# The tail of a two-layer network kernel: y in four 1 MB loads, x1 fetched earlier, four PSUM banks, sixteen result rooms

## The chip, the cores and the metric

The kernel runs on one core of a Trainium2 chip. The metric is the device time of one execution in microseconds; the number given for a kernel is the median of several runs. Beside it there is one profiled execution, whose instructions and transfers are recorded; its span is the time from its first to its last instruction.

## The reference

Two layers, each with a residual. Cut to what matters:

```
x  = x + L0_ffn(L0_cond(x))          # layer 0: (32, 128, 2048), a mixed 128x128 product, then 2048x2048 with LoRA
# layer 1, in the kernel: x1 is the x after layer 0
z  = conv1d_groups4_9taps(x1) + context + bias         # (32, 128, 2048)
t  = z.reshape(4096, 2048)[:, perm] -> (4096, 16 heads, 128)
t  = gelu(t @ up[h]) @ down[h]                         # 128 -> 512 -> 128 for each head
y  = t.reshape(4096, 2048)[:, unperm]
out = x1 + y.reshape(32, 128, 2048)
```

All arithmetic is fp32; products are made as three TensorE products of a high and a low part.

## The kernel before

**Layer 1 in blocks and steps.** The 4096 rows (32 batches of 128 channels) are worked in 8 blocks (`BLOCKS`) of 512 rows, that is 4 batches. A block has 16 steps (`H`), one for each head. In step (k, h) TensorE makes the down products of head h and, between them, the up products of the next head (`down_part` L1336, `up_part` L1326); ScalarE makes gelu and copies y out of PSUM; VectorE splits values into high and low parts (`split_g` L1558, `split_t` L1513). GpSimd gathers the rows of z of a later head from DRAM through the permutation (L1268) and scatters the head's 128 x 512 rows of y to `y_d` in DRAM (L1303). The conv of a later block runs 20 steps ahead (`LEAD`), so the last block has none.

**Final units.** Adding x1 to y and storing is cut into units of one batch and 512 columns, 16 for a block; 256 KB each of y, x1 and output. As y of a block is complete only when its 16 scatters have landed, the units of block k-1 run within block k: SyncE loads y (`load_final`, L1179) and x1 (L1182) two units ahead, TensorE turns y with four 128x128 transposes (`turn_y`, L1371), VectorE adds x1 with a change of the order of columns (`take_final`, L1537), SyncE stores (`store_out`, L1210). SyncE's queue is worked in program order: in each step first a load of the last units' x1 (below), then `load_final`, then `store_out` of two units before. `load_final` of unit v waits for the transposes of v-2 (`fin_done`) and for the sum of v-2 (`o_ready`).

**The tail.** The 16 units of the last block have nothing to hide in. `last_unit(v)` goes through them batch by batch: batch v // 4, columns v % 4.
- x1 (`last_x1[v]`): 7 rooms that are free in the last block are filled by `load_last_x1` (L1192), one in each of its steps 0 to 6, and the other 9 by GpSimd after its last scatter (L1313): four at once into the rooms of gelu, the rest as sums free the first rooms.
- y (`finish`, L1204): after all scatters have landed (wait at L1202), one load of 256 KB for each unit, `y_d[c*512:(c+1)*512, 128 columns]`, so rows of 512 bytes, in a ring of 4 rooms; each waits for the transposes of the unit before its room's last use.
- TensorE turns a unit with four transposes (L1398) into one of two PSUM banks, VectorE adds (L1590) into one of four result rooms, and ScalarE's queue stores it (L1481). A sum waits until the store of the unit four before has landed.

The weights of layer 1 lie in SBUF throughout, as 8 tiles `w_hi[c]` and 8 `w_lo[c]` of 128 x 4 x 512; tile c holds the up and down chunks of heads 2c and 2c+1. So in the last block tile c is read for the last time in step 2c+1.

Of the kernel before, what the change touches and what calls it, by code (L numbers as in the profile page):

```python
# [967 lines left out]
def layer1_block(nc, sh, x1_d, up, down, perm, ident, z_d, y_d, out):  # L968

    with ExitStack() as ctx:  # L970
# [47 lines left out]
        x1_in = [sem(f"x1f_in{j}") for j in range(2)]  # L1018
        fin_done, o_ready = sem("fin_done"), sem("o_ready")
        o_out = [sem(f"o_out{j}") for j in range(2)]  # L1020
        last_x1_in = [sem(f"last_x1_in{v}") for v in range(H)]
        last_yt_in, last_o_out = [sem(f"last_yt_in{j}") for j in range(4)], [sem(f"last_o_out{j}") for j in range(4)]
        last_fin, last_o = sem("last_fin"), sem("last_o")
        block = ctx.enter_context(nc.Block())

# [20 lines left out]
        def drive(eng, step):  # L1046
# [11 lines left out]
            for k in (BLOCKS - 2, BLOCKS - 1):  # L1058
# [3 lines left out]
            step(BLOCKS, 1, 0)  # L1062


        left = ([sh.x1_s[:].rearrange("p a n -> p (a n)")[:, n * 512:(n + 1) * 512] for n in range(4)]
                + [xp[j][:, 0:512] for j in range(2)] + [z_s[:]])
        last_x1 = left + [g_s[:, mc, :] for mc in range(MC)]
        ROOMS = len(last_x1)
        last_x1 = (last_x1 + last_x1)[:H]
        last_x1 = [room.rearrange("p (s q) -> p s q", s=S) for room in last_x1]  # L1070
        last_yt = yt_s + [t.rearrange("p (l r) -> p l r", l=4) for t in t_s]
        last_sum = o_s + [x1.rearrange("p s q -> p (s q)") for x1 in x1_s]
        last_ps = [ps_f[:, 0, :], ps_c[:, 0, :]]

        def last_unit(v):

            return NB - SB + v // 4, v % 4

        def lead(k):
            return isinstance(k, int) and k < 0  # L1080
# [74 lines left out]
        @block.sync  # L1155
        def _(sp):
            sp.dma_start(id_s[:], ident).then_inc(small_in, 16)
            sp.dma_start(idx[:], perm).then_inc(small_in, 16)

            def load_x1(k, h):  # L1160
                u, _, b, g = conv_unit(k, h)

                wait(sp, xlo_ready, u - 3 if isinstance(u, int) and u < H + 2 else u - 1)
                j = xp_of(k, h)
                sh.load_group(sp, x1_d, xp[j], j, b, g)

            def load_final(k, h, parity):
                v, j, b, c = final_unit(k, h)
                if h == 0:
                    scattered = 16 * (H // 2) * k  # L1170
                    if not isinstance(k, int):
                        scattered = sp.snap(scattered)
                    wait(sp, y_out[0], scattered)
                    wait(sp, y_out[1], scattered)
                    sp.sem_inc(block_scattered, 1)
                if isinstance(k, int) and v == 0:
                    sp.wait_ge(z_out[1], 64 * 2)
                wait(sp, fin_done, v - 1)
                sp.dma_start(yt_s[j], y_d[1 - parity][c * 512:(c + 1) * 512, h // 4 * C:(h // 4 + 1) * C]  # L1179
                             .rearrange("(l p) r -> p l r", p=P)).then_inc(yt_in[j], 16)  # L1180
                wait(sp, o_ready, v - 1)
                sp.dma_start(x1_s[j], x1_d[b, :, :, c * P:(c + 1) * P]).then_inc(x1_in[j], 16)  # L1182

            def load_last_x1(v):
                b, c = last_unit(v)
                if v == 0:
                    for j in range(2):
                        sp.wait_ge(z_out[j], 64 * (NB // 2))
                elif v == 4:
                    sp.wait_ge(xlo_ready, STEPS)  # L1190
                    sp.wait_ge(zt_done, STEPS)
                sp.dma_start(last_x1[v], x1_d[b, :, :, c * P:(c + 1) * P]).then_inc(last_x1_in[v], 16)  # L1192

            def finish():

                for j in range(2):
                    sp.wait_ge(y_out[j], 16 * (STEPS // 2))
                sp.wait_ge(tlo_ready, STEPS)
                for v in range(H):
                    b, c = last_unit(v)  # L1200
                    if v < 2:
                        sp.wait_ge(fin_done, STEPS - H - 1 + v)  # L1202
                    wait(sp, last_fin, v - 3)
                    sp.dma_start(last_yt[v % 4], y_d[(BLOCKS - 1) % 2][c * 512:(c + 1) * 512, v // 4 * C:(v // 4 + 1) * C]  # L1204
                                 .rearrange("(l p) r -> p l r", p=P)).then_inc(last_yt_in[v % 4], 16)

            def store_out(k, h):
                v, j, b, c = final_unit(k, h)
                sp.wait_ge(o_ready, v + 1)
                sp.dma_start(out[b, :, c * 512:(c + 1) * 512], o_s[j]).then_inc(o_out[j], 16)  # L1210

            def store_z(k, h, parity):

                u = conv_unit(k, h)[0] - 2
                jb = (h + LEAD - 2) // G % SB
                ahead = (h + LEAD - 2) // G // SB
                if jb == 0:
                    wait(sp, tlo_ready, H * (k + ahead - 1))
                    sp.sem_inc(block_gathered, 1)
                sp.wait_ge(zt_ready, u + 1)  # L1220
                for w in range(4):
                    sp.dma_start(z_d[(parity + ahead) % 2][w * 512:(w + 1) * 512, jb * C:(jb + 1) * C]  # L1222
                                 .rearrange("(q r) n -> q r n", r=S), zt_of(*before(k, h, 2))[:, w, :, :]).then_inc(z_out[jb % 2], 16)

            def step(k, h, parity):
                u = H * k + h + LEAD
                if lead(k) and u < H - 2:
                    load_x1(*after(*after(*after(*after(k, h)))))
                elif lead(k) and u >= H:
                    load_x1(*after(*after(k, h)))  # L1230
                if exists(k, h, LEAD - 2) and (h + LEAD - 2) % G == G - 1:
                    store_z(k, h, parity)
                if not lead(k) and exists(k, h, LEAD + 2):
                    load_x1(*after(*after(k, h)))
                if isinstance(k, int) and k == BLOCKS - 1 and h < len(left):
                    load_last_x1(h)
                if final_exists(k, h, 0):
                    load_final(k, h, parity)
                if final_exists(k, h, 2):
                    store_out(*before(k, h, 2))  # L1240

            sp.wait_ge(sh.pad_ready, 7)
            load_x1(-2, 2 * H - LEAD + 2)
            load_x1(-2, 2 * H - LEAD + 3)
            for p in range(2):
                for blk in range(4):
                    sp.wait_ge(sh.r_out[p][blk], 16 * QUADS)
            drive(sp, step)
            finish()
            sp.wait_ge(o_out[0], 16 * ((STEPS - H) // 2))  # L1250
            sp.wait_ge(o_out[1], 16 * ((STEPS - H) // 2))

        @block.gpsimd
        def _(pool):
# [51 lines left out]

            drive(pool, step)

            pool.wait_ge(glo_ready, MC * STEPS)
            for v in range(len(left), H):  # L1310
                b, c = last_unit(v)
                wait(pool, last_o, v - ROOMS + 1)
                pool.dma_start(last_x1[v], x1_d[b, :, :, c * P:(c + 1) * P]).then_inc(last_x1_in[v], 16)  # L1313
            pool.wait_ge(y_out[0], 16 * (STEPS // 2))
            pool.wait_ge(y_out[1], 16 * (STEPS // 2))

# [1 line left out]
        def _(pe):  # L1318
# [70 lines left out]

            drive(pe, step)  # L1390
            for v in range(H):
                pe.wait_ge(last_yt_in[v % 4], 16 * (v // 4 + 1))
                if v == 0:
                    pe.wait_ge(o_ready, STEPS - H)
                    pe.wait_ge(z_ready, STEPS)
                wait(pe, last_o, v - 1)
                for l in range(4):
                    mm = nc.tensor.transpose(last_ps[v % 2][:, l * P:(l + 1) * P], last_yt[v % 4][:, l, :], id_s[:])  # L1398
                mm.then_inc(last_fin, 1)

        @block.scalar
        def _(act):
# [75 lines left out]
            for v in range(H):  # L1478
                b, c = last_unit(v)
                act.wait_ge(last_o, v + 1)  # L1480
                act.dma_start(out[b, :, c * 512:(c + 1) * 512], last_sum[v % 4]).then_inc(last_o_out[v % 4], 16)  # L1481
            for j in range(4):
                act.wait_ge(last_o_out[j], 16 * (H // 4))

        @block.vector
        def _(dve):
# [96 lines left out]
            dve.wait_ge(o_ready, STEPS - H)  # L1583
            for v in range(H):
                dve.wait_ge(last_fin, v + 1)
                dve.wait_ge(last_x1_in[v], 16)
                if v < 2:
                    dve.wait_ge(o_out[v], 16 * ((STEPS - H) // 2))
                wait(dve, last_o_out[v % 4], 16 * (v // 4))
                nc.vector.tensor_tensor(last_sum[v % 4].rearrange("p (q s) -> p q s", s=S),  # L1590
                                        last_ps[v % 2].rearrange("p (q s) -> p q s", s=S),
                                        last_x1[v].rearrange("p s q -> p q s"), ALU.add).then_inc(last_o, 1)


def build(nc, x, cond_t, fside, w0, b0, w1, b1, w2, b2, cond_w, bias_k, w_t, bias, lora_a, lora_b, coeffs, scales,
# [68 lines left out]
```

## Time and profile before

| | |
|---|---|
| median of 3 runs | 2654.36 us (2651.6 to 2655.67) |
| the profiled execution's time | 2651.15 us |
| its span | 2649.3 us |
| TensorE busy | 2577.4 us, 97% of the span |
| VectorE, ScalarE, GpSimd busy | 1833.2, 1002.2, 959.6 us |
| mean granted TensorE clock | 0.987 of full speed |
| DMA | 541.03 MB, mean 204 GB/s |

In the rows below, names of tiles are those of the SBUF or DRAM tensor that holds the data: `rear` and `u_s` hold the rooms of y, `x_d` is x1 in DRAM, `results` and `rear` the sums, `kern` the gelu values. PE is TensorE, PEld its weight loads, DVE VectorE, ACT ScalarE, POOL GpSimd, SP SyncE; SPq and ACTq are the issue of transfers on those engines. A number behind L is a line of the kernel. Idle time of an engine costs nothing unless the chain of waits goes through it.

### The profile page before, as it was taken

To read this page: it belongs to the slowest core of one execution; us is meant where nothing else is said; L and a number is where in the kernel's file an instruction comes from. 1 tells how busy PE (TensorE), PEld (TensorE's weight loads), DVE (VectorE), ACT (ScalarE), POOL (GpSimd) and SP (SyncE) were. 2 spreads that over 40 slices of the span, in tenths; PEclk is the share of its full clock that TensorE was granted. 3 is DMA by queue.
4 is the path that set the end of the run, shared out by engine and by line. 5 is a ranking of instruction groups with operands and counts; after the bars stand their busy time and mean duration, and the time that the engine had idled before them with its cause. 6 is when DMAs were issued, how large, how long until landed. Compare 5 with 4: busy or idle time off the path is not lost. (4 is left out here: it accounts for less than half of the span.)

```text
span 2649.3 us, 39124 instructions
## 1 busy us (share of the span) xinstructions
PE 2577.4 (97%) x12090; PEld 2112.5 (80%) x12090; DVE 1833.2 (69%) x2671; ACT 1002.2 (38%) x1631; POOL 959.6 (36%) x835
## 2 busy tenths in 40 slices
PE   8899999999999999999999999999999999999896
PEld 6678888888888888888888778888888888888774
DVE  6555555866555755576444767888888888888785
ACT  3211212312122322232222555555555555555572
POOL 2265645456553454233233212222222222222231
PEclk9999999999999999999999999999999999999996
DMA  9855544755545777576455754577777676767677
GB/s 308 308 180 181 198 167 146 262 191 199 181 161 183 224 226 221 159 247 206 151 163 183 216 151 132 171 219 212 221 219 221 209 222 211 228 206 223 182 242 239
DMA packets 419586, 541.03 MB, mean 204 GB/s; under 512 B 36440, under 2 KB 273840, under 8 KB 419376
## 3 DMA queue, kind: packets, MB, share of 16 engines
q1 hardware_dynamic: 317168, 305.04, 38.7%
q10 hardware_dynamic: 77376, 154.27, 15.5%
q0 software_dynamic: 24832, 79.16, 9.5%
q8 instruction: 102, 1.67, 0.3%
q14 instruction: 108, 0.88, 0.1%
HBM read 309.72 MB, written 228.61 MB: 203 GB/s over the span
## 5 line engine op out<-in xcount | busy, mean ns | idle before, releaser
L427 PE MATMUL ps_c<-w_hi,ring_hi 128*128 128x512 f32 x1792 | 714.3, 399 | 10.0 <-DVE ring_lo L910 5.2
L427 PE MATMUL ps_c<-w_hi,ring_lo 128*128 128x512 f32 x1792 | 708.6, 395 | 0.0
L427 PE MATMUL ps_c<-w_lo,ring_hi 128*128 128x512 f32 x1792 | 708.5, 395 | 0.0
L574 ACT ACTIVATE ring_hi<-raw_n 128x512 fp32r<-128x512 f32 x384 | 241.0, 631 | 899.3 <-DVE raw_n L871 247.2
L1303 POOL DMA_INDIRECT y_d<-y_s,idx x128 | 147.1, 1149 | 737.4 <-ACT y_s L1473 676.2
L427 PEld LDWEIGHTS ps_c<-w_hi,ring_hi 128*128 128x128 f32 x1792 | 338.5, 189 | 89.0 <-DVE ring_lo L910 10.9
L1440 ACT ACTIVATE kern<-ps_up 128x512 f32<-128x512 f32 x512 | 306.6, 599 | 261.4 <-PE ps_up L1326 247.0
L427 PEld LDWEIGHTS ps_c<-w_hi,ring_lo 128*128 128x128 f32 x1792 | 338.2, 189 | 79.6
L427 PEld LDWEIGHTS ps_c<-w_lo,ring_hi 128*128 128x128 f32 x1792 | 338.4, 189 | 76.8
L1558 DVE TENSOR_TENSOR g_lo<-kern,g_hi 128x512 fp32r<-128x512 f32 x512 | 354.7, 693 | 40.8 <-ACT g_hi L1444 24.5
L931 DVE TENSOR_TENSOR r_early<-ps_c,r_early 128x512 f32<-128x512 f32 x256 | 176.7, 690 | 285.0 <-PE ps_c L427 285.0
L910 DVE TENSOR_TENSOR ring_lo<-raw_n,ring_hi 128x512 fp32r<-128x512 f32 x384 | 343.1, 894 | 27.9 <-ACT ring_hi L574 27.6
L931 DVE TENSOR_TENSOR x_s<-ps_c,x_s 128x512 f32<-128x512 f32 x192 | 132.5, 690 | 211.8 <-PE ps_c L427 208.1
L1553 DVE CAST g_hi<-kern 128x512 fp32r<-128x512 f32 x474 | 202.7, 428 | 86.6 <-ACT kern L1440 80.5
L691 POOL TENSOR_TENSOR s<-raw_n 128x512 f32<-128x512 f32 x64 | 84.8, 1325 | 442.4 <-DMA raw_n<-u_d 317.8
L1336 PE MATMUL ps_y<-g_hi,w_hi 128*128 128x512 f32 x512 | 213.7, 417 | 6.4 <-ACT y_s L1473 6.4
L1336 PE MATMUL ps_y<-g_hi,w_lo 128*128 128x512 f32 x512 | 201.7, 394 | 0.0
L1336 PE MATMUL ps_y<-g_lo,w_hi 128*128 128x512 f32 x512 | 200.9, 392 | 0.0
L1326 PE MATMUL ps_up<-t_hi,w_hi 128*128 128x512 f32 x472 | 186.9, 396 | 6.6 <-DVE t_lo L1513 6.6
L1326 PE MATMUL ps_up<-t_hi,w_lo 128*128 128x512 f32 x472 | 185.6, 393 | 0.0
L1326 PE MATMUL ps_up<-t_lo,w_hi 128*128 128x512 f32 x472 | 184.2, 390 | 0.0
L1268 POOL DMA_INDIRECT u_s<-z_d,idx x128 | 129.9, 1015 | 76.7 <-issue 38.4
(199 smaller groups left out, 3852.8 us busy)
## 6 DMA issues: line engine op xcount, KB each, us to landing
u_d<-raw_n ACTq DMA_DIRECT2D x64, 512.0 KB, 3.2
x_d<-r_early ACTq DMA_DIRECT2D x128, 256.0 KB, 3.4
x_d<-x_s ACTq DMA_DIRECT2D x128, 256.0 KB, 2.6
raw_n<-u_d SPq DMA_DIRECT2D x64, 512.0 KB, 3.5
u_s<-x_d SPq DMA_DIRECT2D x496, 64.0 KB, 2.5
z_d<-x_s SPq DMA_DIRECT2D x120, 256.0 KB, 3.9
rear<-y_d SPq DMA_DIRECT2D x120, 256.0 KB, 3.1
rear<-x_d SPq DMA_DIRECT2D x112, 256.0 KB
```

What stands on the lines that cost most here:

```text
L427: mm = nc.tensor.matmul(bank, a[:, dc, :], w[k][:, dc, :], start=(first and dc == 0 and n == 0), stop=(dc == 3 and n == 2), skip_group_che ...
L574: nc.scalar.activation(ring_hi[g % RING][:].rearrange("p a n -> p (a n)"), ring_raw[p][k], ACT.Copy).then_inc(hi_ready, 1)
L691: nc.gpsimd.tensor_tensor(s1[:, p, :], a21, a22, ALU.add).then_inc(s_ready, 1)
L910: nc.vector.tensor_tensor(ring_lo[g % RING][:].rearrange("p a n -> p (a n)"), ring_raw[p][k], fp32(ring_hi[g % RING][:].rearrange("p a n - ...
L931: nc.vector.tensor_tensor(r_s[p][blk], bank, r_s[p][blk], ALU.add).then_inc((u_read if on_u else y_read)[p], 1)
L1268: nc.gpsimd.indirect_dma_start(out=t_s[j], out_offset=None, in_=z_d[parity], in_offset=bass.IndirectOffsetOnAxis(ap=idx[:, h:h + 1], axis= ...
L1303: nc.gpsimd.indirect_dma_start(out=y_d[parity], out_offset=bass.IndirectOffsetOnAxis(ap=idx[:, h:h + 1], axis=0), in_=y_s[j][:], in_offset ...
L1326: mm = nc.tensor.matmul(ps_up[:, mc, :], chunk(w, 2 * h)[:, mc * P:(mc + 1) * P], t, start=(n == 0), stop=(n == 2))
L1336: mm = nc.tensor.matmul(ps_y[:, 0, :], chunk(w, 2 * h + 1)[:, mc * P:(mc + 1) * P], g[:, mc, :], start=(mc == 0 and w is w_hi and g is g_h ...
L1440: nc.scalar.activation(g_s[:, mc, :], ps_up[:, mc, :], ACT.Gelu).then_inc(gelu_done, 1)
L1553: nc.vector.tensor_copy(g_hi[:, mc, :], g_s[:, mc, :]).then_inc(ghi_ready, 1)
L1558: nc.vector.tensor_tensor(g_lo[:, mc, :], g_s[:, mc, :], fp32(g_hi[:, mc, :]), ALU.subtract).then_inc(glo_ready, 1)
```

## The change

- `finish` loads y with four transfers of 1 MB, one for each group of 512 columns and all four batches: rows of 2 KB. They go to `w_hi[0..3]`, dead by then, and wait for the scatters alone.
- x1 of all 16 last units is fetched by SyncE in the last block: in each of steps 3, 5, 7 and 9 four loads of 256 KB into `w_lo[c]`, c = 0 to 3, behind a wait until step 2c+1's down products are done. GpSimd loads no x1.
- `last_unit` goes through the units by columns first: batch v % 4, columns v // 4.
- The transposes go to four PSUM banks instead of two, and each sum has a room of its own, so no sum waits for a store (the last takes a room of the block before and waits for that one's store).

```diff
-        last_x1 = left + [g_s[:, mc, :] for mc in range(MC)]
-        ROOMS = len(last_x1)
-        last_yt = yt_s + [t.rearrange("p (l r) -> p l r", l=4) for t in t_s]
-        last_sum = o_s + [x1.rearrange("p s q -> p (s q)") for x1 in x1_s]
-        last_ps = [ps_f[:, 0, :], ps_c[:, 0, :]]
+        last_yt, last_x1 = [fp32(w_hi[c][:]) for c in range(4)], [fp32(w_lo[c][:]) for c in range(4)]
+        last_sum = (... 16 rooms: x1_s of layer 0, xp, z_s, t_s, g_s, x1_s, o_s[:1])
+        last_ps = [ps_f[:, 0, :], ps_c[:, 0, :], ps_zt[:, 0, :], ps_up[:, 0, :]]
         def last_unit(v):
-            return NB - SB + v // 4, v % 4
+            return NB - SB + v % 4, v // 4
...
-            def load_last_x1(v):
-                b, c = last_unit(v)
-                if v == 0:
-                    for j in range(2):
-                        sp.wait_ge(z_out[j], 64 * (NB // 2))
-                elif v == 4:
-                    sp.wait_ge(xlo_ready, STEPS)
-                    sp.wait_ge(zt_done, STEPS)
-                sp.dma_start(last_x1[v], x1_d[b, :, :, c * P:(c + 1) * P]).then_inc(last_x1_in[v], 16)
+            def load_last_x1(c):
+                sp.wait_ge(down_done, MC * (STEPS - H + 2 * c + 2))
+                for n in range(4):
+                    sp.dma_start(last_x1[c][:, n, :], x1_d[NB - SB + n, :, :, c * P:(c + 1) * P]).then_inc(last_x1_in[c], 16)
             def finish():
                 for j in range(2):
                     sp.wait_ge(y_out[j], 16 * (STEPS // 2))
-                sp.wait_ge(tlo_ready, STEPS)
-                for v in range(H):
-                    b, c = last_unit(v)
-                    if v < 2:
-                        sp.wait_ge(fin_done, STEPS - H - 1 + v)
-                    wait(sp, last_fin, v - 3)
-                    sp.dma_start(last_yt[v % 4], y_d[(BLOCKS - 1) % 2][c * 512:(c + 1) * 512, v // 4 * C:(v // 4 + 1) * C]
-                                 .rearrange("(l p) r -> p l r", p=P)).then_inc(last_yt_in[v % 4], 16)
+                for c in range(4):
+                    sp.dma_start(last_yt[c], y_d[(BLOCKS - 1) % 2][c * 512:(c + 1) * 512, :]
+                                 .rearrange("(l p) r -> p l r", p=P)).then_inc(last_yt_in[c], 16)
...
-                if isinstance(k, int) and k == BLOCKS - 1 and h < len(left):
-                    load_last_x1(h)
+                if isinstance(k, int) and k == BLOCKS - 1 and h in (3, 5, 7, 9):
+                    load_last_x1((h - 3) // 2)
...
-            pool.wait_ge(glo_ready, MC * STEPS)
-            for v in range(len(left), H):
-                b, c = last_unit(v)
-                wait(pool, last_o, v - ROOMS + 1)
-                pool.dma_start(last_x1[v], x1_d[b, :, :, c * P:(c + 1) * P]).then_inc(last_x1_in[v], 16)
...
-                pe.wait_ge(last_yt_in[v % 4], 16 * (v // 4 + 1))
-                wait(pe, last_o, v - 1)
+                pe.wait_ge(last_yt_in[c], 16)
+                wait(pe, last_o, v - 3)
                 for l in range(4):
-                    mm = nc.tensor.transpose(last_ps[v % 2][:, l * P:(l + 1) * P], last_yt[v % 4][:, l, :], id_s[:])
+                    mm = nc.tensor.transpose(last_ps[v % 4][:, l * P:(l + 1) * P], last_yt[c][:, l, b * C:(b + 1) * C], id_s[:])
...
-                act.dma_start(out[b, :, c * 512:(c + 1) * 512], last_sum[v % 4]).then_inc(last_o_out[v % 4], 16)
+                act.dma_start(out[b, :, c * 512:(c + 1) * 512], last_sum[v]).then_inc(last_o_out, 16)
...
-                dve.wait_ge(last_x1_in[v], 16)
-                wait(dve, last_o_out[v % 4], 16 * (v // 4))
+                dve.wait_ge(last_x1_in[c], 16 * 4)
```

## Rows read from the trace of the kernel before

**Rows 1.** The page: the span of the profiled execution.
```profile
span 2649.3 us, 39124 instructions
```
**Rows 2.** The chain that ended last, in the tail: start, length in us, what.
```profile
2607.57 3.26 DMA y_d<-y_s,idx
2610.90 6.41 DMA rear<-y_d
...
2621.79 10.76 DMA u_s<-y_d
...
2645.74 1.02 DVE rear L1590
```
**Rows 3.** Timeline of the tail: start, length in us, instruction, idle before it.
```profile
2617.35 1.11 PE L1398 MATMUL ps_f<-id_s,rear 128*128 128x128 f32 x4 [10.52 <-DMA rear<-y_d]
...
2618.56 1.03 DVE L1590 TENSOR_TENSOR results<-ps_f,x_s 128x512 f32<-128x512 f32 x1 [10.67 <-PE ps_f L1398]
2619.50 1.03 DVE L1590 TENSOR_TENSOR results<-ps_c,x_s 128x512 f32<-128x512 f32 x1
...
2627.34 1.02 DVE L1590 TENSOR_TENSOR results<-ps_c,u_s 128x512 f32<-128x512 f32 x1 [3.14 <-DMA out_dram<-results]
```
**Rows 4.** Windows of the tail: us, busy by engine, granted clock, DMA share, GB/s.
```profile
2611.00:2617.00 6.00, 0.00 (x0) 0.00 (x0) 0.00 (x0) 0.00 (x0) 0.61 (x1) 0.50 0.96 281
...
2624.00:2630.00 6.00, 1.30 (x5) 0.72 (x4) 1.70 (x3) 0.00 (x0) 0.75 (x1) 0.50 0.99 346
...
2642.00:2649.30 7.30, 2.83 (x11) 1.62 (x9) 3.16 (x4) 0.00 (x0) 0.00 (x0) 0.50 0.58 212
```
**Rows 5.** DMA queues from 2608 on (SP, ACT, POOL): packets, MB, share of engines.
```profile
q1 hardware_dynamic: 8592, 4.46, 38.0%
q10 hardware_dynamic: 2304, 4.20, 27.3%
q0 software_dynamic: 800, 2.62, 22.0%
```
**Rows 6.** Single transfers of the tail, issue to landing: loads at 2610.9, 2612, 2623.2; last store.
```profile
rear<-y_d SPq DMA_DIRECT2D x1, 256.0 KB, 6.4
...
u_s<-y_d SPq DMA_DIRECT2D x1, 256.0 KB, 7.1
...
rear<-y_d SPq DMA_DIRECT2D x1, 256.0 KB, 10.8
...
out_dram<-rear ACTq DMA_DIRECT2D x1, 256.0 KB, 2.0
```
**Rows 7.** Single transfers at the run's start, in order of issue on SP's queue.
```profile
u_s<-in_lora_b SPq DMA_DIRECT2D x1, 512.0 KB, 3.9
...
raw_n<-in_lora_b SPq DMA_DIRECT2D x1, 512.0 KB, 6.7
...
x_s<-in_w_t SPq DMA_DIRECT2D x1, 512.0 KB, 8.3
```
**Rows 8.** The 1 MB weight loads of layer 0 (L599, 21 of them).
```profile
DMA to landing us min/median/max: 5.1/7.8/10.9
```
**Rows 9.** Windows: a stretch of layer 0's opening.
```profile
60.00:70.00 10.00, 9.55 (x43) 7.60 (x42) 7.28 (x9) 3.11 (x6) 0.00 (x0) 1.00 1.01 372
```
**Rows 10.** Windows: two stretches of the last block.
```profile
2510.00:2516.00 6.00, 6.00 (x21) 4.67 (x20) 2.65 (x6) 3.19 (x6) 0.29 (x1) 0.70 0.66 195
...
2520.00:2530.00 10.00, 10.00 (x47) 7.73 (x46) 7.75 (x14) 7.96 (x15) 2.47 (x3) 1.00 1.05 325
```
**Rows 11.** Timeline of the last block: y load of unit 3, an x1 load, unit 3's transposes.
```profile
2522.63 0.36 SPq L1179 DMA_DIRECT2D rear<-y_d  x1
...
2526.74 0.55 SPq L1192 DMA_DIRECT2D u_s<-x_d  x1
...
2534.44 0.60 PE L1371 MATMUL ps_f<-id_s,rear 128*128 128x128 f32 x4
```
**Rows 12.** The y load issued at 2522.63, issue to landing.
```profile
rear<-y_d SPq DMA_DIRECT2D x1, 256.0 KB, 5.0
```

More of the change, by code:

```diff
@@ L1020, in layer1_block @@
         o_out = [sem(f"o_out{j}") for j in range(2)]
-        last_x1_in = [sem(f"last_x1_in{v}") for v in range(H)]
-        last_yt_in, last_o_out = [sem(f"last_yt_in{j}") for j in range(4)], [sem(f"last_o_out{j}") for j in range(4)]
+        last_x1_in, last_yt_in = [sem(f"last_x1_in{c}") for c in range(4)], [sem(f"last_yt_in{c}") for c in range(4)]
+        last_o_out = sem("last_o_out")
         last_fin, last_o = sem("last_fin"), sem("last_o")
@@ L1062, in drive @@
             step(BLOCKS, 1, 0)
-        left = ([sh.x1_s[:].rearrange("p a n -> p (a n)")[:, n * 512:(n + 1) * 512] for n in range(4)]
-                + [xp[j][:, 0:512] for j in range(2)] + [z_s[:]])
-        last_x1 = left + [g_s[:, mc, :] for mc in range(MC)]
-        ROOMS = len(last_x1)
-        last_x1 = (last_x1 + last_x1)[:H]
-        last_x1 = [room.rearrange("p (s q) -> p s q", s=S) for room in last_x1]
-        last_yt = yt_s + [t.rearrange("p (l r) -> p l r", l=4) for t in t_s]
-        last_sum = o_s + [x1.rearrange("p s q -> p (s q)") for x1 in x1_s]
-        last_ps = [ps_f[:, 0, :], ps_c[:, 0, :]]
+        last_yt, last_x1 = [fp32(w_hi[c][:]) for c in range(4)], [fp32(w_lo[c][:]) for c in range(4)]
+        last_sum = ([sh.x1_s[:].rearrange("p a n -> p (a n)")[:, n * 512:(n + 1) * 512] for n in range(4)]
+                    + [xp[j][:, 0:512] for j in range(2)] + [z_s[:]] + t_s + [g_s[:, mc, :] for mc in range(MC)]
+                    + [x1.rearrange("p s q -> p (s q)") for x1 in x1_s] + o_s[:1])
+        last_ps = [ps_f[:, 0, :], ps_c[:, 0, :], ps_zt[:, 0, :], ps_up[:, 0, :]]
         def last_unit(v):
-            return NB - SB + v // 4, v % 4
+            return NB - SB + v % 4, v // 4
         def lead(k):
@@ L1391, in _ @@
             for v in range(H):
-                pe.wait_ge(last_yt_in[v % 4], 16 * (v // 4 + 1))
+                b, c = v % 4, v // 4
+                pe.wait_ge(last_yt_in[c], 16)
                 if v == 0:
@@ L1395, in _ @@
                     pe.wait_ge(z_ready, STEPS)
-                wait(pe, last_o, v - 1)
+                    pe.wait_ge(zt_ready, STEPS)
+                    pe.wait_ge(gelu_done, MC * STEPS)
+                wait(pe, last_o, v - 3)
                 for l in range(4):
-                    mm = nc.tensor.transpose(last_ps[v % 2][:, l * P:(l + 1) * P], last_yt[v % 4][:, l, :], id_s[:])
+                    mm = nc.tensor.transpose(last_ps[v % 4][:, l * P:(l + 1) * P], last_yt[c][:, l, b * C:(b + 1) * C], id_s[:])
                 mm.then_inc(last_fin, 1)
@@ L1480, in _ @@
                 act.wait_ge(last_o, v + 1)
-                act.dma_start(out[b, :, c * 512:(c + 1) * 512], last_sum[v % 4]).then_inc(last_o_out[v % 4], 16)
-            for j in range(4):
-                act.wait_ge(last_o_out[j], 16 * (H // 4))
+                act.dma_start(out[b, :, c * 512:(c + 1) * 512], last_sum[v]).then_inc(last_o_out, 16)
+            act.wait_ge(last_o_out, 16 * H)
         @block.vector
@@ L1585, in _ @@
                 dve.wait_ge(last_fin, v + 1)
-                dve.wait_ge(last_x1_in[v], 16)
-                if v < 2:
-                    dve.wait_ge(o_out[v], 16 * ((STEPS - H) // 2))
-                wait(dve, last_o_out[v % 4], 16 * (v // 4))
-                nc.vector.tensor_tensor(last_sum[v % 4].rearrange("p (q s) -> p q s", s=S),
-                                        last_ps[v % 2].rearrange("p (q s) -> p q s", s=S),
-                                        last_x1[v].rearrange("p s q -> p q s"), ALU.add).then_inc(last_o, 1)
+                b, c = v % 4, v // 4
+                dve.wait_ge(last_x1_in[c], 16 * 4)
+                if v == 0:
+                    for j in range(2):
+                        dve.wait_ge(z_out[j], 64 * (NB // 2))
+                if v == H - 1:
+                    dve.wait_ge(o_out[0], 16 * ((STEPS - H) // 2))
+                nc.vector.tensor_tensor(last_sum[v].rearrange("p (q s) -> p q s", s=S),
+                                        last_ps[v % 4].rearrange("p (q s) -> p q s", s=S),
+                                        last_x1[c][:, b, :].rearrange("p (s q) -> p q s", s=S), ALU.add).then_inc(last_o, 1)
 def build(nc, x, cond_t, fside, w0, b0, w1, b1, w2, b2, cond_w, bias_k, w_t, bias, lora_a, lora_b, coeffs, scales,
```

## The prediction

> **What bounds the kernel now.** I read the page first: one execution spans 2649.3 us [rows 1]. Then the chain of waits of the end, because only the last block and the tail are touched. Up to 2606 us the chain is TensorE's matmuls. From there it is the tail: the last scatter of y lands 3.26 us after its issue at 2607.57, and from 2610.90 on the chain is mostly loads of y, 6.41 us for the first and one link of 10.76 us in the middle; only the last link is a VectorE sum that starts at 2645.74 [rows 2]. So the tail (2610.9 to 2649.3, 38.4 us) waits for transfers. The timeline of the tail shows what the engines need when data is there: a unit's four transposes take some 1.1 us, the sum follows 1.2 us after their start, and sums follow one another at 0.94 us (2618.56, 2619.50); one sum waits 3.14 us for a room whose store is under way [rows 3]. 16 units at 0.94 to 1.03 us are 15 to 16.5 us: less than half of the tail.
>
> The windows of the tail show the DMA engines at a share of 0.96 to 0.99 in the middle, but at 281 GB/s in one stretch and 346 in another, and 0.58 at the end [rows 4]. The table of queues says why the rate varies: SP's queue moved 4.46 MB in 8592 packets (519 B each, 38.0% of the 16 engines' time, 29 ns a packet, so 284 GB/s if it had all engines), ACT's stores 4.20 MB in 2304 packets (27.3%, 78 ns each, 372 GB/s), and POOL's queue carried another 2.62 MB, mostly x1 [rows 5]. A y load in the tail landed after 6.4 us when x1 ran beside it and after 10.8 us when x1 and stores did; the last store, alone, after 2.0 us [rows 6].
>
> **The change, part by part.**
>
> *x1 leaves the tail.* Nine loads of 256 KB (2.36 MB) on POOL's queue go. In their place 16 loads (4.19 MB) on SP's queue run in the last block instead of 7. In the tail this takes the queue away that shares the engines with y.
>
> *y in 2 KB rows.* 16 loads with 512 B rows become 4 of 1 MB with 2 KB rows, issued together. Nothing gates them but the last scatter, as before: 2610.90. SP's other waits there (the last split, old rooms) are over by then, so removing them gives nothing. The first lands when? The very first loads of the run, 512 KB each and issued on one queue one after another, landed after 3.9, 6.7 and 8.3 us [rows 7]: a queue finishes its transfers in order. 3.9 us plus another 0.52 MB at 360 GB/s (1.5 us) is 5.4 us. The 1 MB weight loads of the first layer, under other traffic, took 5.1 at least and 7.8 us in the median [rows 8]. I take 5.4, so 2616.3; bounds 5.1 and 7.8.
>
> *Four banks, 16 rooms.* A sum waits no more for a store, and transposes run three units ahead. This removes the 3.14 us wait and those behind the gating of y by old rooms (SP's next y loads waited for transposes). TensorE and VectorE do the same work with the same access patterns, so 1.1 and 1.03 us an instruction group stay.
>
> *Two floors of the new tail.* Compute: 2616.3, plus 1.2 to the first sum, plus 15 steps of 0.95, plus the last sum 1.03, 0.1 to its store and 2.0 to land: 2634.9 (2636.1 at 1.03 a step). Transfers: 4.19 MB in and 4.19 MB out are 8.39 MB. For their rate the nearest rows are the tail's 346 GB/s, held down by 512 B rows, the 372 that ACT's packets give, and a stretch of the first layer with large rows in both directions, 372 GB/s at a share of 1.01 [rows 4, 5, 9]. I take 360: 23.3 us. Bounds 346 (24.2) and 385, a little above the best row (21.8). To this come 2.5 us in which nothing of it moves: 512 KB took 3.9 us, of which 1.4 is moving. 2610.9 + 23.3 + 2.5 = 2636.7. The two floors nearly meet. Loads and stores have equal packets now and share about evenly; with stores at 256 KB per 0.95 us the fourth y load lands near 2628.5, when 11 units are summed, so compute hardly waits. The later floor decides: 2636.7, I say 2637 for joints. Gain 2649.3 - 2637 = 12.3 us.
>
> The Trainium skill (DMA: Bandwidth & Descriptors, section "Measured", loads issued from GpSimd) gives 341 GB/s for a 1 MB transfer and more for larger ones; by it 8.39 MB would take 24.6 us, 1.3 us more than I take. No row here shows a lone 1 MB load.
>
> *The last block pays or hides.* The added load is 9 x 256 KB = 2.36 MB, 4608 packets of 512 B; at 29 ns and 16 engines that is 8.4 us of all engines spread over 93 us. It comes in bursts of 1 MB at steps 3, 5, 7, 9. SP, before them, waits until the second step of each pair has ended on TensorE. That is about the moment at which it issued the y load of the step anyway (2522.63 for unit 3), so the wait itself costs nothing. Four issues of 0.55 us follow, and behind them stand the y load, the x1 load and the store of the running unit: the y load is issued at about 2524.9 instead of 2522.63, and needed by the transposes at 2534.44 [rows 11]. It took 5.0 us before [rows 12]. Behind 1 MB of 512 B packets (3.7 us at 284 GB/s) beside a scatter and a gather (0.5 MB, 1.5 us) it lands at 2524.9 + 5.0 + at most 3.7 - what the removed early loads free: 2531 to 2533.6. It fits by 1 to 3 us. The ten microseconds from 2520 had a DMA share of 1.05 and 325 GB/s before, with TensorE busy 10.00 of 10.00 [rows 10]: full engines did not stall it. The later bursts meet emptier stretches (2540 on). The gathers are on POOL, not behind SP; they share engines only. So I cost the block at 0; if the cover went, each burst would cost what the y load is late, 0 to 4 us, and a lower clock behind it: after the stall near 2507 TensorE was granted 0.70 of full speed for six microseconds [rows 10], some 2 us.
>
> **Sum.** 0 in the block, 12.3 us gained in the tail. The profiled execution took 2651.15 us, 1.85 beside its span, which the change does not touch; it becomes 2638.9. The three timed runs have 2654.36 in the median (2651.6 to 2655.67), 3.2 above. I put the gain on the median: 2642.
>
> **Rivals.**
> 1. *y loads land together* (12%). If the four 1 MB transfers advance side by side and not in turn, the first lands near 2610.9 + 2.0 + 4.19 MB at 370 = 2624.2, and all compute comes after: + 1.2 + 14.25 + 1.03 + 2.1 = 2642.8 to 2643.5. Gain about 6, time 2648.5. For it: the tail's first four y loads, issued within 2 us, had latencies of 6.4 to 7.1, hardly apart [rows 6]. Against it: the climbing 3.9, 6.7, 8.3 [rows 7]; and the four shared their engines with x1 of POOL's larger packets, gone now. The Trainium skill (same page, "Queues, rings and completion order") says that completion is not FIFO per issuing engine, though each ring is consumed in order; that speaks for this rival only in part.
> 2. *The bursts nibble* (10%). One or two of four y loads come late by 1 to 4 us, with the clock loss: 2 to 8 us back. Time 2644 to 2650.
> 3. *The block stalls and it ends slower* (5%). The mechanism is the y load of units 3, 5, 7, 9 behind the burst. It turns the sign when the four stalls exceed 12.3 us, 3.1 each, and to be slower by over 0.2% they must reach 17.6, 4.4 each. With 1 to 3 us of margin the load must land some 12 to 14 us after issue. A y load did take 10.8 us in the tail, beside x1 and stores [rows 6]. With 4.5 us per burst and 1.5 of clock: +24 - 12.3, time 2666. Against it: before, 1.05 shares cost at most 5.0 us for this load [rows 12].
> 4. *The transfers bound the tail at the old rate* (6%). If 8.39 MB move at 281 GB/s [rows 4], they take 29.9 us: end 2643.3, gain 6, time 2648.4; with gaps of 2 or 3 us no measurable change.
>
> **Numbers.** The forecast has 67%, its own range is 2637 to 2645: compute floor 2634.9 gives 2640, the best execution lies 2.8 below the median, so 2637; above, 7.8 us to the first landing adds 2.4. 0.2% is 5.3 us, about what a measurement of this kernel tells from no change: the border is 2649. The forecast, most of 2 and half of 1 and 4 are faster: 0.84; the other half of 1 and 4 and a bit of 2 are the same: 0.10; slower 0.06. The range for 8 in 10 takes in rivals 1 and 4: 2637 to 2649.5.
>
> **What would show it.** First y load issued at about 2611 and its transposes 5 to 6 us later (rival 1: 12). Sums at 0.95 us steps, 16 of them within some 17 us; no wait of a sum for a store; DMA share near 1 until the end, packets of about 2 KB on both queues, no POOL transfer in the tail. Last sum to end about 2 us before the span ends. In the block: TensorE busy 10 of 10 in each stretch from 2520 on, no wait of the running unit's transposes for y. A row there of several us, or a last scatter later than 2607.57 by as much, proves rival 2 or 3. A tail of 26 us is the forecast; 32 refutes it.

## The result and the profile after

The changed kernel takes 2638.65 us in the median of 4 runs (2636.86 to 2641.66), the kernel before 2654.46 (2651.6 to 2655.67): ratio 0.9943, 95% interval 0.9926 to 0.9960. A second comparison on one chip gave 2637.59 against 2651.81, ratio 0.9943 (0.9929 to 0.9956). It is faster, by 0.57% where 0.47% was forecast. The profiled execution spans 2638.5 us.

The chain that ended last, in the tail of the changed kernel (start, length in us, what; DVEq is VectorE's instruction queue):

```profile
2609.31 3.13 DMA y_d<-y_s,idx
2612.51 5.57 DMA w_hi<-y_d
2618.13 1.13 PE ps_f L1383 x4
...
2620.30 0.72 DVE x_s L1577
2625.09 0.93 DVE z_s L1577
...
2631.81 0.93 DVEq L970
2632.74 0.93 DVE rear L1577
2633.67 0.93 DVE results L1577
```

This answers to [rows 2]. One load of y is left in it, 5.57 us, and behind it the chain is VectorE's sums. I call *tail* the time from the first y load's issue to the end of the span: 38.4 us before (2610.90 to 2649.3), 26.0 now (2612.51 to 2638.5). The timeline shows the first and the last sums:

```profile
2612.51 2.45 SPq L1191 DMA_DIRECT2D w_hi<-y_d  x4
2619.34 1.05 DVE L1577 TENSOR_TENSOR x_s<-ps_f,w_lo 128x512 f32<-128x512 f32 x1 [9.73 <-PE ps_f L1383]
2620.30 1.04 DVE L1577 TENSOR_TENSOR x_s<-ps_c,w_lo 128x512 f32<-128x512 f32 x1
...
2632.66 1.01 DVE L1577 TENSOR_TENSOR rear<-ps_zt,w_lo 128x512 f32<-128x512 f32 x1
2633.60 1.01 DVE L1577 TENSOR_TENSOR results<-ps_up,w_lo 128x512 f32<-128x512 f32 x1
```

From the first start to the last there are 14.26 us for 15 steps, 0.95 each; after the first one no sum has an idle time in brackets (four of the 16 are shown). In [rows 3] one waited 3.14 us for a store. The windows, in the columns of [rows 4] and [rows 10] (us; busy time of TensorE, its weight loads, VectorE, ScalarE and GpSimd; granted clock; DMA share; GB/s): three stretches of the last block, then the tail.

```profile
2520.00:2530.00 10.00, 10.00 (x46) 7.84 (x46) 8.13 (x14) 7.39 (x14) 2.93 (x3) 1.00 1.04 324
...
2530.00:2540.00 10.00, 10.00 (x47) 7.82 (x46) 8.33 (x14) 6.85 (x13) 3.93 (x4) 1.00 0.98 304
...
2560.00:2570.00 10.00, 10.00 (x48) 7.69 (x47) 8.32 (x14) 7.61 (x14) 3.17 (x4) 1.00 0.94 292
...
2611.00:2617.00 6.00, 0.00 (x0) 0.00 (x0) 0.00 (x0) 0.00 (x0) 0.00 (x0) 0.66 0.64 214
2617.00:2624.00 7.00, 5.87 (x32) 5.88 (x32) 4.66 (x5) 0.00 (x0) 0.00 (x0) 0.56 1.02 370
2624.00:2630.00 6.00, 4.02 (x27) 2.52 (x25) 6.00 (x8) 0.00 (x0) 0.00 (x0) 1.00 1.05 390
2630.00:2638.50 8.50, 1.25 (x8) 0.84 (x8) 4.60 (x5) 0.00 (x0) 0.00 (x0) 0.70 0.78 296
```

TensorE is busy 10.00 of 10.00 in these stretches of the block although the DMA share is 0.94 to 1.04. In the six microseconds from 2624 VectorE is busy 6.00 of 6.00 and the DMA share is 1.05 at the same time: both floors are reached. Cut where the bytes begin and end to move, the tail has three parts:

```profile
2612.51:2614.50 1.99, 0.00 (x0) 0.00 (x0) 0.00 (x0) 0.00 (x0) 0.00 (x0) 0.59 0.29 41
2614.50:2636.50 22.00, 11.15 (x64) 9.24 (x64) 15.27 (x16) 0.00 (x0) 0.00 (x0) 0.73 1.01 377
2636.50:2638.50 2.00, 0.00 (x0) 0.00 (x0) 0.00 (x0) 0.00 (x0) 0.00 (x0) 0.50 0.05 17
```

For 22 of the 26 us the DMA engines are full, at 377 GB/s; in the other 4 us almost nothing moves. The queues of the end (SP's, ACT's, POOL's, as [rows 5]) and the landing of the four y loads (least, median, most):

```profile
q1 hardware_dynamic: 2400, 4.72, 43.5%
q10 hardware_dynamic: 2304, 4.20, 36.4%
q0 software_dynamic: 80, 0.26, 2.3%
```

```profile
DMA to landing us min/median/max: 5.6/8.9/13.8
```

SP's queue now has packets of about 2 KB (4.72 MB in 2400; 4.19 MB of it are y), and POOL's has only the last scatter.

### The profile page after: what moved, and what is told of

The parts are those of the page before. It is cut to its first block and busy times, and to the rows that moved or that the text cites. A ratio compares the mean times of both kernels' runs of the same rounds, so it can differ in the third digit from the quotient of the medians.

```text
span 2638.5 us, 39106 instructions
## 1 busy us (share of the span) xinstructions
PE 2570.8 (97%) x12090; PEld 2111.6 (80%) x12090; DVE 1837.5 (70%) x2671; ACT 1001.5 (38%) x1631; POOL 955.3 (36%) x826
## 5 line engine op out<-in xcount | busy, mean ns | idle before, releaser
L1255 POOL DMA_INDIRECT u_s<-z_d,idx x128 | 130.1, 1016 | 76.6 <-issue 38.4
```

Of the source, the lines that this page charges most:

```text
L1255: nc.gpsimd.indirect_dma_start(out=t_s[j], out_offset=None, in_=z_d[parity], in_offset=bass.IndirectOffsetOnAxis(ap=idx[:, h:h + 1], axis= ...
```

## The experiments

All tails are read the same way as above. "Block" is the time from the issue of the scatter of step 1 of the last block to that of its last scatter: 84.3 us before (2523.25 to 2607.57) and after (2524.98 to 2609.31). Whole runs of one kernel mostly spread over 4 to 8 us, and in the profiles most of that lies in the part ahead of the tail. So small effects are read from tails, each from one profile. The two profiles of the changed kernel agree to 0.1 us in the tail, but the run without x1 loads below, whose tail has the same work, is 0.7 us shorter in it. So a difference under about 0.7 us shows nothing. Where a run's time is not given, it was timed once and only its tail or block is read.

**One part at a time, on the kernel before: x1 alone.**

```diff
-        last_x1 = left + [g_s[:, mc, :] for mc in range(MC)]
+        last_x1 = [fp32(w_lo[c][:]) for c in range(4)]
...
-                    load_last_x1(h)                # steps 0 to 6, the rest by GpSimd in the tail
+                    load_last_x1((h - 3) // 2)     # steps 3, 5, 7, 9: four loads each
```

> The kernel before, with one part of the change: x1 of all 16 last units goes into the low weight tiles during the last block, as in the changed kernel; y still comes in 16 gated loads of 256 KB, two banks, four rooms. I call tail the time from the first y load of the end to the end of the span: 38.4 us before, 26.0 after. Theory (transfers share the engines, POOL's x1 starves the 512 B rows of y): tail 31 to 33, and no stall in the block. Rival (the tail's length is the gating of y loads and sums by old rooms): tail 36 or more.

2643.83 us against 2650.88, ratio 0.9970 (0.9957 to 0.9982). Tail 29.7 us (2612.39 to 2642.1), 8.7 less than before and below the theory's 31. This is about what the bytes of the nine loads cost at the tail's mean rate: it moves 279 GB/s before and 283 here, and 2.36 MB at 280 are 8.4 us. Against the 360 GB/s of the prediction it would be 6.6. What SP's queue got (packets, MB, share of the engines) in the six microseconds from 2624, before the change and here:

```profile
q1 hardware_dynamic: 1045, 0.52, 29.6%
q1 hardware_dynamic: 2136, 1.06, 59.8%
```

With x1 and the stores beside it y had 29.6% of the engines' time; without x1 it has twice that, and twice the bytes. The chain of this kernel shows what comes forward then:

```profile
2618.80 1.05 DVE rear L1579
2619.87 4.91 DMA out_dram<-rear
2624.91 1.04 DVE rear L1579
2625.97 5.68 DMA out_dram<-rear
2631.77 1.03 DVE rear L1579
2632.82 4.58 DMA out_dram<-rear
```

It waits for stores: the result rooms are the next limit.

**Large y loads alone.**

```diff
-        last_yt = yt_s + [t.rearrange("p (l r) -> p l r", l=4) for t in t_s]
+        last_yt = [fp32(w_hi[c][:]) for c in range(4)]
...
-                for v in range(H):                 # 16 loads of 256 KB, gated
+                for c in range(4):                 # 4 loads of 1 MB
```

> The kernel before, with y in four ungated 1 MB loads into the high weight tiles and the units ordered by columns; x1 as before (9 of 16 loads on POOL in the tail), two banks, four rooms. Theory: 10.75 MB still have to move, tail 30 to 33. Rival (row size and gating of y are all of it): 26 to 28.

2649.4 against 2650.88, ratio 0.9991 (0.9982 to 1.0001). Tail 35.6 us (2611.17 to 2646.8): only 2.8 gained, worse than both guesses (single loads of y now land 9.6 to 19.1 us after their issue). The chain:

```profile
2611.17 9.56 DMA w_hi<-y_d
2620.77 1.13 PE ps_f L1393 x4
2621.98 1.04 DVE results L1585
...
2624.28 1.04 DVE rear L1585
2625.35 8.38 DMA out_dram<-rear
```

With x1 on POOL's queue beside it, the first 1 MB lands after 9.56 us, where the changed kernel has 5.57, and a store after 8.38; with four rooms that store stops the sums.

**Banks and rooms alone.**

```diff
-        last_sum = o_s + [x1.rearrange("p s q -> p (s q)") for x1 in x1_s]
-        last_ps = [ps_f[:, 0, :], ps_c[:, 0, :]]
+        last_sum = [x1.rearrange("p s q -> p (s q)") for x1 in x1_s] + [y[:] for y in y_s] + o_s
+        last_ps = [ps_f[:, 0, :], ps_c[:, 0, :], ps_zt[:, 0, :], ps_up[:, 0, :]]
...
```

> The kernel before, with four PSUM banks instead of two and six result rooms instead of four; y and x1 as before. Theory: sums wait mostly for y, so 37 to 38.5 us. Rival (rooms and banks set the pace): 33 to 35.

These are six result rooms instead of four. Tail 37.6 us (2616.47 to 2654.1), 0.8 less, as the theory had it and hardly more than the noise. No sum waits for a store now, but transposes go on waiting for y: those into `ps_f` alone 11.8 us.

**The changed kernel with the old banks and rooms.**

```diff
-                wait(pe, last_o, v - 3)
+                wait(pe, last_o, v - 1)
...
+                wait(dve, last_o_out[v % 4], 16 * (v // 4))
-                nc.vector.tensor_tensor(last_sum[v].rearrange("p (q s) -> p q s", s=S),
-                                        last_ps[v % 4].rearrange("p (q s) -> p q s", s=S),
+                nc.vector.tensor_tensor(last_sum[v % 4].rearrange("p (q s) -> p q s", s=S),
+                                        last_ps[v % 2].rearrange("p (q s) -> p q s", s=S),
...
```

> The changed kernel with two banks and four result rooms, as before the change. A store lands 3.7 to 6.5 us after its issue in the changed kernel. Theory: four rooms then turn over in about 6 us, 1.5 us a unit instead of 0.95, tail 29 to 32. Rival (rooms are worth nothing): 26.

Tail 32.2 us (2613.39 to 2645.6), just above the theory's 32. Its timeline of VectorE:

```profile
2623.54 1.04 DVE L1577 TENSOR_TENSOR x_s<-ps_c,w_lo 128x512 f32<-128x512 f32 x1
2628.44 1.02 DVE L1577 TENSOR_TENSOR x_s<-ps_f,w_lo 128x512 f32<-128x512 f32 x1 [3.85 <-DMA out_dram<-x_s]
2629.38 1.03 DVE L1577 TENSOR_TENSOR x_s<-ps_c,w_lo 128x512 f32<-128x512 f32 x1
2630.73 1.04 DVE L1577 TENSOR_TENSOR x_s<-ps_f,w_lo 128x512 f32<-128x512 f32 x1 [0.32 <-PE ps_f L1383]
...
2636.42 1.02 DVE L1577 TENSOR_TENSOR x_s<-ps_f,w_lo 128x512 f32<-128x512 f32 x1 [1.38 <-DMA out_dram<-x_s]
```

Two waits for stores, 5.2 us, and 0.32 us at the five other changes from one pair of banks to the next, 1.6 us, make most of the 7.4 us by which its 15 steps are longer (21.7 us against 14.3). From the start of its last sum to the end of the span are 3.6 us instead of 4.9, which gives 1.3 back. So banks and rooms are worth 0.8 us where transfers come late and 6.2 us where they don't.

This kernel is also the first one, x1 alone, with large y loads added: 32.2 us against 29.7. With four rooms the large loads make the tail 2.5 us longer. Its first sum starts 6.9 us after the first y load's issue, in the kernel with x1 alone 4.1. The three parts of the change cannot be added up one by one: only with more banks and rooms do the large loads stop costing.

**y in 16 small loads, ungated** (no load waits for transposes).

```diff
-                for c in range(4):
-                    sp.dma_start(last_yt[c], y_d[...][c * 512:(c + 1) * 512, :] ...)
+                for v in range(H):
+                    sp.dma_start(last_yt[c][:, :, b * C:(b + 1) * C], y_d[...][c * 512:(c + 1) * 512, b * C:(b + 1) * C] ...)
```

> The changed kernel with y in 16 loads of 256 KB (512 B rows), all issued at once, each unit with its own semaphore; x1, banks and rooms as changed. Theory (512 B packets cost 29 ns each and share badly with 2 KB packets): the first sum starts about 2 us earlier, but 8192 such packets and the stores need 26 us of all engines, tail 28 to 30. Rival (only number and gating of loads mattered): 24 to 26.

Tail 27.8 us (2609.10 to 2636.9): between the two guesses, 1.8 more than the changed kernel. The first sum starts 4.25 us after the first issue instead of 6.83, and SP's packets take more of the engines for fewer bytes (window 2608 to 2637):

```profile
2613.35 1.03 DVE L1578 TENSOR_TENSOR x_s<-ps_f,w_lo 128x512 f32<-128x512 f32 x1 [7.16 <-PE ps_f L1384]
```

```profile
q1 hardware_dynamic: 8448, 4.20, 51.9%
q10 hardware_dynamic: 2304, 4.20, 39.4%
```

The early start is lost again: later transposes wait for y, and two sums wait 2.3 and 2.6 us for them. The seven microseconds from 2623 have 348 GB/s at a share of 1.11, where the changed kernel has 390 at 1.05 from 2624. The loads are not issued at once either: SyncE needs 17.64 us for the 16. This run doesn't separate the cost of the packets from that.

**No x1 loads at all.** The last units add what lies in the tiles.

```diff
-                if isinstance(k, int) and k == BLOCKS - 1 and h in (3, 5, 7, 9):
-                    load_last_x1((h - 3) // 2)
```

> The changed kernel without any load of the last units' x1: the last 16 units add what the tiles hold, so their part of the output is wrong. It shows what the four 1 MB bursts cost the last block. Theory: nothing; from the scatter of step 1 to the last scatter 84.3 us with them (2524.98 to 2609.31) and 84.1 to 84.5 without. Rival (hidden losses in the block): 2 us less. Tail 26 either way.

Block 84.3 us (2525.33 to 2609.67), the same to 0.02 us. The four bursts cost the block nothing. The tail is 25.3 us (2612.88 to 2638.2), where the same work took 26.0 and 26.1. Its last sum starts 21.06 us after the first y load's issue, as in the changed kernel (21.09); only the end behind it is shorter, and nothing in the edit explains that.

**One burst of 4 MB.**

```diff
-                ... and h in (3, 5, 7, 9):
-                    load_last_x1((h - 3) // 2)
+                ... and h == 9:
+                    for c in range(4):
+                        load_last_x1(c)
```

> The changed kernel with all 16 x1 loads issued at step 9 of the last block in one burst of 4 MB. Theory: the y load behind it has some 12 us from issue to use and now 4 MB at about 300 GB/s, 14 us, before it: TensorE stalls once for 3 to 8 us, so the margin that the spread bursts keep is real. Rival (queues never hurt the block): no stall.

The block takes 96.4 us (2525.10 to 2621.49): 12.1 lost, more than the 3 to 8 expected, and the kernel is at 2652.38 us, no faster than before (2650.7, one run each). The tail is unchanged, 25.8. SyncE's queue shows why it is more:

```profile
2559.60 17.11 SPq L1184 DMA_DIRECT2D w_lo<-x_d  x16
2576.76 1.00 SPq L1175 DMA_DIRECT2D rear<-y_d  x1
```

In bursts of four a load takes 0.64 us to issue (2.57 us for four), here 1.07. Each of the 16 landed 4.5 to 7.2 us after its issue, at a DMA share of 1.06: SyncE issues them no faster than they move. The y load is issued only behind all of them. TensorE stands idle for 9.5 us before that unit's transposes:

```profile
2583.22 1.12 PE L1354 MATMUL ps_f<-id_s,rear 128*128 128x128 f32 x4 [9.49 <-DMA rear<-y_d]
```

and the ten microseconds from 2580 have a granted clock of 0.56 in their mean. So rival 3 of the prediction is a real mechanism; the spread bursts stay clear of it. Most of the delay here lies in the issue, which the prediction had priced at 0.55 us a load.

**Faster sums.** The last sums are written without the change of column order (the last units' output is in the wrong order).

```diff
-                nc.vector.tensor_tensor(last_sum[v].rearrange("p (q s) -> p q s", s=S), ...
+                nc.vector.tensor_tensor(last_sum[v], last_ps[v % 4], last_x1[c][:, b, :], ALU.add)
```

> The changed kernel with the last 16 sums written without the change of column order (output of these units in the wrong order), which takes some 0.65 us instead of 1.03. It takes VectorE's floor away. Theory (VectorE's pace and the transfers nearly meet, transfers end 24 to 25 us after the first y load): tail 24 to 25. Rival (VectorE alone sets the tail): 21 to 22. Rival 2 (transfers alone): 26.

A sum takes 0.69 us instead of 1.03, and the tail 25.8 (2612.41 to 2638.2): 0.2 less, which is noise. Rival 2 of this run, transfers alone, is what came out; my 24 to 25 was wrong. The last sum starts 18.3 us after the first y load's issue instead of 21.1, and the span ends 7.5 us behind it instead of 4.9: the stores are queued up. They start earlier, and the last y load lands after 14.2 us instead of 13.8:

```profile
2628.18 0.66 PE L1383 MATMUL ps_f<-id_s,w_hi 128*128 128x128 f32 x4 [2.16 <-DMA w_hi<-y_d]
```

**A smaller first load.**

```diff
-                for c in range(4):
+                for n, (c, b, many) in enumerate(((0, 0, 1), (0, 1, 1), (0, 2, 2), (1, 0, 4), (2, 0, 4), (3, 0, 4))):
```

> The changed kernel with the first 1 MB load of y cut into 256, 256 and 512 KB (rows of 512 B, 512 B, 1 KB) on the same queue, each with its own semaphore, so that the first sum can start sooner. Theory after the run with plain sums (VectorE's pace and the transfers both end near 26 us): sums start 2 to 2.5 us earlier, but the same 8.39 MB have to pass, tail 25.0 to 25.8. Rival (the chain of sums alone sets the tail): 23.5 to 24.

2639.24 us, ratio 0.9948 (0.9934 to 0.9961) against 0.9943 for the changed kernel in the same comparison. Tail 26.5 us (2613.17 to 2639.7): no gain, a miss again. The first sum starts 4.08 us after the first issue, 2.75 earlier than in the changed kernel, but the third one waits for its y, the fifth again for 1.45 us, and the last one starts 22.9 us after the first issue instead of 21.1:

```profile
2618.20 1.01 DVE L1579 TENSOR_TENSOR x_s<-ps_c,w_lo 128x512 f32<-128x512 f32 x1
2622.21 1.03 DVE L1579 TENSOR_TENSOR x_s<-ps_zt,w_lo 128x512 f32<-128x512 f32 x1 [3.00 <-PE ps_zt L1385]
```

**Both.** The split and the plain sums together.

> The split first load together with the plain sums (last units' output in the wrong order): both remedies for a late or slow VectorE at once. Theory (transfers end the tail): 25.0 to 25.8, no better than the split alone. Rival: 20 to 22.

Tail 26.3 us (2610.66 to 2637.0), no shorter either: with VectorE's start and its pace both bettered, the transfers hold the tail near 26.

**The changed kernel again.**

> The changed kernel once more, beside the kernel before on the same chip, for the time. The tails differ by 12.4 us, the block by nothing; executions of one kernel spread over 5 us. If the tail is all of it the ratio is 0.9953 within its interval; the first result's 0.9943 would be that plus noise of the part before the last block. Rival (the part before the last block has become faster too): 0.994 or less again, with an interval that leaves 0.9953 out.

Ratio 0.9943 (0.9929 to 0.9956), tail 26.1 us (2611.20 to 2637.3). The interval holds 0.9953, so this run doesn't settle whether anything but the tail became faster.

## Why the prediction was right

*x1 leaves the tail* is the largest part: alone it gives 8.7 us of the 12.4. That x1 takes the engines from y is borne out: in a window of six microseconds y's share of them doubles without it, from 29.6% to 59.8%, and the first 1 MB load lands after 9.56 us beside x1 and 5.57 without. That small packets of y are what suffers is not shown by this: the 9.56 us were measured with packets of 2 KB. For small packets in a tail without x1 there is only the net 1.8 us of the kernel with 16 small loads, its earlier start included.

*First landing:* 5.4 forecast, 5.57 measured; the four landed 5.6, 7.8, 9.9 and 13.8 us after their issues, so the loads come in turn and rival 1 is out. The Trainium skill's sentence (DMA: Bandwidth & Descriptors, "Queues, rings and completion order") that completion is not FIFO per issuing engine had no effect here: nothing else is issued on this queue beside them, and the spread of 5.6 to 13.8 shows the loads one after another.

*Compute floor:* first sum after 6.6, then 14.25 us to the last: measured 6.83 and 14.26. The end was mis-sized: the last store lands after 3.4 us, not 2.0. The store before it was issued 1 us earlier and needed some 2.9 us, so it was still under way; before the change it was alone. From the last sum's end to the span's end are 3.9 us against 2.1 forecast. So this floor was forecast at 24.0 us and came out at 26.0: in the changed kernel it is not the lower of the two.

```profile
out_dram<-results ACTq DMA_DIRECT2D x1, 256.0 KB, 3.4
```

*Transfer floor:* 25.8 forecast from 8.39 MB at 360 GB/s and 2.5 us; with the compute floor lifted, the runs gave 25.8 and 26.3. Both terms were off, in opposite directions: the full stretch of 22 us moves 377 GB/s, more than 360, and the parts in which almost nothing moves are 4 us, not 2.5 (22.0 + 4.0 against 23.3 + 2.5). By the Trainium skill's 341 GB/s for a load of 1 MB (DMA: Bandwidth & Descriptors, "Measured") an estimate, with the same 2.5 us, would have been 27.1; the trace's 377 is higher, for loads and stores together.

*The two floors meet:* right, and closer than forecast: 26.0 by the sums, 25.8 and 26.3 by the transfers. It explains why neither faster sums nor an earlier start helps, and why rooms were worth 6.2 us at the end of the row of edits and 0.8 at its start. That last point the prediction missed: it listed the store waits as a small term (3.14 us seen before), while under faster loads they and the two banks would have cost 6.2.

*The block:* costed at 0, measured 0.0 in two ways. The y load of unit 3 was issued at 2525.84 and its transposes ran at 2536.17 in step. That is 10.3 us from issue to use, where it was 11.8 before (2522.63 to 2534.44) and 9.5 forecast. When the load landed isn't in the trace, so the margin itself was not measured; the single burst only shows that it ends somewhere between 1 and 4 MB.

*The time:* tail 12.3 us shorter forecast, 12.4 measured. That the two agree to 0.1 us is luck: errors of 1.3 and 1.5 us nearly cancel in one floor, the other was 2.0 us too low, and tails of equal work differ by 0.7. The mechanism was right. The profiled span fell by 10.8 because its last scatter came 1.74 us later than before (2609.31 against 2607.57); the medians fell by 15.8 and 14.2. So the median came out 3.4 us below the 2642 that was forecast. The 1.8 and 3.4 us beyond the tail are within the intervals, and no profile shows the part before the last block faster. Whether they are more than the spread of runs stays open.

## What to carry to other kernels

When a tail waits for transfers, add up its bytes and its compute separately before editing: the later of the two floors is what it can reach, and an edit is worth what it takes off the present limit, so buffers that are worth next to nothing today (0.8 us) may be worth 6.2 after the next edit, and large loads that cost 2.5 us with few buffers may gain with more. Move loads whose data is long complete into the loaded but not late stretch before, in pieces small enough that what stands behind them in the same queue still arrives. Take loads that can run earlier away from beside those that the end waits for; the DMA engines' time is shared between them. Judge such an edit by its own stretch of the profile when the rest of the run is noisier than the gain.

## What the runs showed of the hardware that was not expected

TensorE's clock rose in the changed tail. Before the change it stood at 0.50 of full speed (1.2 GHz) in every stretch read from 2611 to the end, three of them in [rows 4]. Now transposes run without a pause from 2618.13 on, and from about 2623 they are at full speed, 2.4 GHz: the window from 2624 has 1.00, though TensorE is busy only 4.02 of its 6 us. By the timeline a unit's four transposes fall from 1.06 to 0.63 us:

```profile
2620.74 1.06 PE L1383 MATMUL ps_up<-id_s,w_hi 128*128 128x128 f32 x4
...
2624.35 0.63 PE L1383 MATMUL ps_f<-id_s,w_hi 128*128 128x128 f32 x4
```

It gave nothing: at the lower clock units of transposes started 0.85 us apart (2619.04, 2619.89, 2620.74), already faster than VectorE's sums at 0.95.

SyncE can be held in issuing: 2.57 us for four loads of 256 KB with 512 B rows, 17.11 us for sixteen x1 loads in a row and 17.64 for sixteen of y. In both of the latter the DMA share was 1.0 or more (1.06 and 1.01), so the issue kept to the pace of the transfers, and what stands behind them is late before it is issued.
